# Layer 0 of a two-layer graph network: a buffer of its own for the second table's rows, their split behind the router, loop values loaded a step ahead, and one gate's products behind the turned sums

## The chip, the cores and the metric

The kernel runs on one core of a Trainium2 chip. The metric is the device time of one execution in microseconds (us). An execution is one launch that computes everything below.

## The reference, cut to what matters

There are 6250 nodes with 256 features, and 100,000 edges sorted by their target. The targets are drawn as 6250 times a uniform number squared, so that low node numbers get many more edges than high ones.

```
x = x + GRU(sum over edges of (LN(x)[src] + rel[type]), LN(x))          # layer 0, graph part
x = x + shared_mlp(LN(x)) + top-2-of-4 experts_mlp(LN(x))               # layer 0, feed forward part
x = x + (sum over edges of LN(x)[src]) @ W.T / (degree + 1) + ...       # layer 1, graph part
x = x + top-2-of-8 experts of gelu MLPs on LN(x)                        # layer 1, feed forward part
```

## The kernel before

Nodes are cut into 49 tiles of 128. A table of normalised rows lies in HBM (`table1` for layer 0, `table2` for layer 1). GpSimd (POOL) walks once over the edges in chunks of 128 (784 chunks, four to a block) and gathers one row of the table per edge with an indirect DMA (L763) into `rows`, a ring of 8 blocks. Before a block it waits until TensorE (PE) has used the block that held the slot before (`free`), and it tells PE when blocks have landed (`ready`, L751).

For each tile ("window") VectorE (DVE) builds a one-hot matrix per edge chunk (`dve_onehots`, L789 and L793), and PE multiplies it with the gathered rows and sums into a PSUM bank (`pe_window`, L814 to L836). The number of blocks of a window is data: PE and DVE load it, and the place of the window in the ring, from SBUF into registers (`value_load`) and then run a loop over the blocks. PE needs two loads for a window; DVE needs three for the first 8 blocks of a window, and one with a branch for the blocks behind them (`late`). ScalarE (ACT) and DVE then empty the bank (`act_empty` L1293 and L1296, `dve_empty` L1307).

Tiles are worked on in groups: one tile, then eleven groups of four, then two of two, from the highest tile to the lowest. The dense work of group g-1 is cut into steps d1 to d5, and an order written out by hand (`run_graph`) puts one window of group g behind each of the steps d1 to d4 of group g-1, on every engine the same way. d1 is the GRU (PE turns the sums with L953 and L957, ACT copies them with L1092, and the gate products L934 follow), d2 turns the new state back, adds it to `x_res` and normalises into `h4` (L1224), d3 holds the router and the first two layers of the feed forward part, and d4 its third layer, the second layer norm into `h4` again, and the turning of the next group's `h4_in`. d5 splits that `h4` into two f16 halves in `part`: the high one on ACT (L1151), the low one on DVE (L1281). ACT then sends `part` to `table2` (L1154) and waits for `lo_done` before it does. d5 of group g-2 stands behind the first window of group g, so between d1 and d2 of group g-1.

Each engine runs its own instructions in order. Layer 1 begins behind a barrier that ends layer 0; it gathers from `table2` in the same way with another set of steps.

Of the kernel before, what the change touches and what calls it, by code (L numbers as in the profile page):

```python
# [23 lines left out]
ds = bass.ds  # L24
# [47 lines left out]
def program(nc, a, out):  # L72
# [6 lines left out]
    with ExitStack() as ctx:  # L79
# [25 lines left out]
        place = sb("place", [P, NT * 2], I32)  # L105
        to_list = sb("to_list", [P, LCOLS], I32)
        from_list = sb("from_list", [P, LCOLS], I32)
# [136 lines left out]
        part = sb("part", [P, GW, PARTS * D], F16, layer0)  # L244

# [99 lines left out]
        with nc.Block() as block:  # L345
# [35 lines left out]
            def _(pool):  # L381
# [7 lines left out]
                nc.gpsimd.iota(place[:, :], pattern=[[P, NT], [0, 2]], base=1, channel_multiplier=1)  # L389
# [380 lines left out]

        def dve_onehots(dve, q, t, late):

            if late:
                blocks = dve.value_load(windows[0:1, ds(t + NT, 1)], min_val=1, max_val=PASS + 1)
                with dve.If(blocks > MH):
                    dve_onehots_of(dve, q, t, MH, blocks)
            else:
                dve_onehots_of(dve, q, t, 0, dve.value_load(early[0:1, ds(t, 1)], min_val=1, max_val=MH))

        def dve_onehots_of(dve, q, t, j0, j1):  # L780
            before = dve.snap(window_first(dve, t) + t)
            first = narrow(dve.value_load(windows[0:1, ds(t + 2 * NT, 1)]), 0, PASS)
# [137 lines left out]
        def pe_d1(pe, g, w):  # L920
# [38 lines left out]
            last.then_inc(S["redT_ps"], 1)  # L959

# [23 lines left out]
        def pe_d2(pe, g, w):  # L984
            pe.wait_ge(S["deg_sb"], g + 1)
            for c in range(C):
                pe.wait_ge(S["hnew"], 2 * g + c + 1)
                for half, lo, k in halves(w):
                    for i in range(lo, lo + k):
                        o = (i - lo) * D + c * P  # L990
                        last = nc.tensor.transpose(bank[3 + half][:, o:o + P], nT[:, c, i * P:(i + 1) * P], ident[:, :])
                    if c == C - 1:
                        last.then_inc(S["back_ps"], per_half(w))

        def pe_d3(pe, g, w):
            n = w * P
            for i in range(w):
# [30 lines left out]
        def pe_d4(pe, g, w):  # L1028
            n = w * P
            pe.wait_ge(S["gates_ready"], g + 1)  # L1030
# [116 lines left out]
        def act_d5(act, g, w):  # L1147
            act.wait_ge(S["table2_out"], 16 * g + 16)
            act.wait_ge(S["h2_ready"], g + 1)
            for half, lo, k in halves(w):  # L1150
                nc.scalar.activation(part[:, lo:lo + k, 0:D], h4[:, lo:lo + k, :],  # L1151
                                     ACT.Copy).then_inc(S["hi_done"], per_half(w))
            act.wait_ge(S["lo_done"], CREDIT + 2 * g + 2)
# [20 lines left out]
        def dve_d1(dve, chain, g, w):  # L1174
# [30 lines left out]
        def dve_d2(dve, chain, g, w):  # L1205
# [15 lines left out]
            if not (isinstance(g, int) and g == 0):  # L1221
                dve.wait_ge(S["hi_done"], CREDIT + 2 * g)
# [29 lines left out]
        def dve_d4(dve, chain, g, w):  # L1252
# [20 lines left out]
            ln_apply(first_tile(g), w).then_inc(S["h2_ready"], 1)  # L1273
# [4 lines left out]
        def dve_d5(dve, chain, g, w):  # L1278
            for half, lo, k in halves(w):
                dve.wait_ge(S["hi_done"], CREDIT + 2 * g + half + 1)  # L1280
                nc.vector.tensor_tensor(part[:, lo:lo + k, D:2 * D], h4[:, lo:lo + k, :],  # L1281
# [28 lines left out]
        def nothing(g, w):  # L1310
            return None

# [44 lines left out]
        with nc.Block() as block:  # L1357
# [5 lines left out]
            def _(pe):  # L1363
                pe.sem_inc(q1.used, MH)
                run_graph(lambda g, i: pe_windows(pe, q1, g, i, None),
                          [lambda g, w, f=f: f(pe, g, w) for f in (pe_d1, pe_d2, pe_d3, pe_d4)] + [nothing], pe)

            @block.scalar
            def _(act):
# [4 lines left out]
                run_graph(lambda g, i: act_emptied1(act, g, i),  # L1374
                          [lambda g, w, f=f: f(act, g, w) for f in (act_d1, act_d2, act_d3, act_d4, act_d5)], act)
# [3 lines left out]
            def _(dve):  # L1379
                chain = Chain(dve, "layer0_chain", 64)  # L1380
                for at in (G_ONE, G_AGAIN + E0):
# [3 lines left out]
                run_graph(dve_gather(dve, q1, evacuate1),  # L1385
                          [lambda g, w, f=f: f(dve, chain, g, w) for f in (dve_d1, dve_d2, dve_d3, dve_d4, dve_d5)], dve)
# [5 lines left out]
        ffn = ctx.enter_context(ExitStack())  # L1392

# [75 lines left out]
        low_f = sb("low_f", [P, 2 * GW], F32, layer1)  # L1469
        place_f = sb("place_f", [P, NT * 2], F32, layer1)  # L1470
# [123 lines left out]
        def dve_e3(dve, chain, g, w):  # L1594
# [18 lines left out]
            if isinstance(g, int) and g == 0:  # L1613
                dve.wait_ge(R["cols_ready"], 2)
# [25 lines left out]
        with nc.Block() as block:  # L1640
# [12 lines left out]
            def _(pool):  # L1653

                nc.gpsimd.iota(from_list[:, :], pattern=[[1, LCOLS]], base=0,
# [6 lines left out]
            def _(pe):  # L1662
                pe.sem_inc(q2.used, MH)
                steps = [lambda g, w: pe_e0(pe, g, w), lambda g, w: pe_e1(pe, g, w), lambda g, w: pe_e2(pe, g, w), lambda g, w: pe_e3(pe, g, w), nothing]
# [14 lines left out]
            def _(dve):  # L1679
# [7 lines left out]
                dve.wait_ge(R["cols_ready"], 1)  # L1687
# [4 lines left out]
                chain = Chain(dve, "layer1_chain", 64)  # L1692

# [318 lines left out]
```

## Time and profile before

| what | us |
|---|---|
| median of 3 executions without the profiler | 3396.59 (3394.66 to 3401.94) |
| the profiled execution | 3414.43 |
| its span, from the first to the last instruction | 3412.9 |
| PE busy in the span | 2328.8 |
| POOL busy in the span | 1923.9 |

The profiled execution took 17.8 us longer than the median. All rows below come from it. The first gather of layer 0 starts about 112 us into the span, the last ends at 1472, and layer 1 begins at 1520.7.

### The profile page before, as it was taken

The numbers are of one execution on the slowest core, as the hardware profiler recorded it, in microseconds if no ns is written. First come the engines' busy times: TensorE is split into PE (matmuls) and PEld (weight loads), VectorE is DVE, ScalarE is ACT, GpSimd is POOL, SyncE is SP. The second block draws the span as 40 slices with busy tenths as digits, with TensorE's granted clock in tenths as the row PEclk, the third lists the DMA queues.
The fourth block names the chain that finished last, engine by engine and source line by source line (L and its number), as shares of the span: only waits on it lengthen the run. The fifth ranks groups of instructions, "written<-read, shape, count | busy, mean of one in ns | idle before, by whom it ended". The sixth has DMA issues, their size and how long they took to land. (4 is left out here: it accounts for less than half of the span.)

```text
span 3412.9 us, 47179 instructions
## 1 busy us (share of the span) xinstructions
PE 2328.8 (68%) x11708; PEld 1564.6 (46%) x11709; DVE 1532.5 (45%) x4138; ACT 828.9 (24%) x1644; POOL 1923.9 (56%) x2043
## 2 busy tenths in 40 slices
PE   1478999988866775345666555444443389999996
PEld 1245555555443442132333232221111179999996
DVE  7445555555542433123555443332321156666663
ACT  2233333333322211020110000000000035555543
POOL 0364445556666666626666666666666445555553
PEclk6589999999986776566777766665665589999998
DMA  5322222223232323223333333333333443333334
GB/s 166 88 81 67 71 65 79 79 81 89 87 90 81 87 82 88 82 66 90 101 92 99 92 92 95 90 91 92 91 99 89 138 99 72 73 73 71 71 48 106
DMA packets 163077, 298.23 MB, mean 87 GB/s; under 512 B 47543, under 2 KB 106656, under 8 KB 162752
## 3 DMA queue, kind: packets, MB, share of 16 engines
q0 software_dynamic: 96736, 235.19, 26.3%
q1 hardware_dynamic: 41476, 39.54, 3.7%
q10 hardware_dynamic: 24732, 22.06, 2.1%
q8 instruction: 44, 0.72, 0.1%
q14 instruction: 89, 0.73, 0.1%
HBM read 255.78 MB, written 47.27 MB: 89 GB/s over the span
## 5 line engine op out<-in xcount | busy, mean ns | idle before, releaser
L763 POOL DMA_INDIRECT rows<-table,srcT x1568 | 1552.4, 990 | 985.5 <-issue 498.3
L829 PE MATMUL bank<-rows,onehot 128*128 x1952 | 672.7, 486 | 704.4 <-POOLq L751 435.6
L829 PEld LDWEIGHTS bank<-rows,onehot 128*128 x1952 | 218.6, 112 | 1118.8 <-issue 995.6
L789 DVE SCALAR_TENSOR_TENSOR onehot<-iota_row,tbase,dstT 128x512 f16 x488 | 366.6, 753 | 677.8 <-issue 429.2
L1923 ACT ACTIVATE hid<-bank,b 128x256 f32<-128x256 f32 x432 | 178.9, 465 | 291.5 <-PE bank L1875 266.6
L1873 PE MATMUL bank<-W_high,hid_high 128*128 128x256 f32 x864 | 244.9, 283 | 0.0
L1873 PE MATMUL bank<-xe_high,W_high 128*128 128x256 f32 x864 | 241.2, 279 | 4.8 <-DVE xe_low L1956 4.7
L1874 PE MATMUL bank<-xe_low,W_high 128*128 128x256 f32 x864 | 240.0, 278 | 0.0
L1875 PE MATMUL bank<-xe_high,W_low 128*128 128x256 f32 x864 | 240.0, 278 | 0.0
L1874 PE MATMUL bank<-W_low,hid_high 128*128 128x256 f32 x864 | 239.9, 278 | 0.0
L1875 PE MATMUL bank<-W_high,hid_low 128*128 128x256 f32 x864 | 239.9, 278 | 0.0
L1638 ACT ACTIVATE sums<-bank 128x256 f32<-128x256 f32 x49 | 18.8, 383 | 897.8 <-issue 401.8
L1969 DVE TENSOR_TENSOR hid_low<-hid,hid_high 128x512 fp32r<-128x512 f32 x216 | 150.6, 697 | 168.3 <-ACT hid_high L1927 166.8
L1833 POOL DMA_INDIRECT totals<-ys,to_old x112 | 182.9, 1633 | 73.5 <-POOL to_new L1813 49.2
L1824 POOL DMA_INDIRECT xs<-normal,rows_of x110 | 132.4, 1204 | 64.7 <-POOL rows_of L1820 44.4
L1873 PEld LDWEIGHTS bank<-xe_high,W_high 128*128 128x128 f32 x864 | 163.4, 189 | 6.5 <-issue 6.5
L1874 PEld LDWEIGHTS bank<-xe_low,W_high 128*128 128x128 f32 x864 | 163.5, 189 | 0.0
L1875 PEld LDWEIGHTS bank<-xe_high,W_low 128*128 128x128 f32 x864 | 163.4, 189 | 0.0
L1873 PEld LDWEIGHTS bank<-W_high,hid_high 128*128 128x128 f32 x864 | 162.3, 188 | 0.0
L1874 PEld LDWEIGHTS bank<-W_low,hid_high 128*128 128x128 f32 x864 | 162.3, 188 | 0.0
L1875 PEld LDWEIGHTS bank<-W_high,hid_low 128*128 128x128 f32 x864 | 162.2, 188 | 0.0
L1927 ACT ACTIVATE hid_high<-hid 128x512 fp32r<-128x512 f32 x216 | 136.5, 632 | 7.0
(351 smaller groups left out, 3754.0 us busy)
## 6 DMA issues: line engine op xcount, KB each, us to landing
rows<-table,srcT POOLq DMA_INDIRECT x1568
W<-in_L_ffn_W_dram SPq DMA_DIRECT2D x14, 1024.0 KB
x_res<-in_x_dram SPq DMA_DIRECT2D x1, 6144.0 KB, 22.4
normal<-xn ACTq DMA_DIRECT2D x11, 528.0 KB
table<-part ACTq DMA_DIRECT2D x11, 512.0 KB
totals<-x_res SPq DMA_DIRECT2D x11, 512.0 KB, 6.8
table<-part SPq DMA_DIRECT2D x6, 512.0 KB, 2.9
table<-part_b SPq DMA_DIRECT2D x6, 512.0 KB, 2.9
```

What stands on the lines that cost most here:

```text
L763: nc.gpsimd.indirect_dma_start(out=rows[:, k % (M * U), 0:ROW], out_offset=None, in_=q.table, in_offset=bass.IndirectOffsetOnAxis(srcT[:, ...
L789: last = nc.vector.scalar_tensor_tensor(onehot[:, ds(slot, U), :], iota_row[:, :].unsqueeze(1).to_broadcast([P, U, P]), base, dstT[:, ds(k ...
L829: last = nc.tensor.matmul(acc[:, 0:ROW], hots[:, ds(hot0 + s * P, P)], ring_rows[:, ds(row0 + s * ROW, ROW)], start=False, stop=False, ski ...
L1638: nc.scalar.activation(sums4[:, slot_of(g, i), :], acc[:, 0:D], ACT.Copy).then_inc(R["high_out"], 1)
L1824: nc.gpsimd.indirect_dma_start(out=xs[:, s, :], out_offset=None, in_=normal, in_offset=bass.IndirectOffsetOnAxis(rows_of[:, s:s + 1], axis ...
L1833: nc.gpsimd.indirect_dma_start(out=totals, out_offset=bass.IndirectOffsetOnAxis(to_old[:, s:s + 1], axis=0), in_=ys[:, s, :], in_offset=No ...
L1873: nc.tensor.matmul(acc, w_high, m_high, start=start, stop=False)
L1874: nc.tensor.matmul(acc, w_high, m_low, start=False, stop=False)
L1875: return nc.tensor.matmul(acc, w_low, m_high, start=False, stop=stop)
L1923: nc.scalar.activation(hid[:, hc, :], bank[1 + pair][:, o:o + TT], ACT.Gelu, bias=b1[b][:, hc:hc + 1]).then_inc(X["gelu_done"], 1)
L1927: nc.scalar.activation(hid_high[:, both, :], hid[:, both, :], ACT.Copy).then_inc(X["hid_high"], 1)
L1969: nc.vector.tensor_tensor(hid_low[:, both, :], hid[:, both, :], hid_high[:, both, :].bitcast(F32), ALU.subtract).then_inc(X["hid_ready"], 1)
```

## The change

Six edits, all but the last in layer 0.

- The second layer norm writes into a new buffer `h2_4` and no longer into `h4`; d5 reads it. The wait on `hi_done` moves from the writes of `h4` (L1224) to those of `h2_4`.
- d5 of group g-2 moves from between d1 and d2 of group g-1 to between d3 and d4, behind the third window. The wait for `lo_done` and the DMA to `table2` become a step of their own (d6) behind the fourth window.
- PE loads the two values of each window of the next group ahead: those of window 0 in d1 behind the hidden products, and those of windows 1, 2 and 3 at the head of d2, d3 and d4 (for groups of four tiles).
- DVE loads the three values for the one-hots of window 1 right behind the one-hots of window 0, inside d1.
- The six hidden products of gate r, half 1 (bank 1) move from ahead of the turned sums to behind them.
- The index buffers `place`, `to_list` and `from_list` are taken from SBUF later, and the iota of `place` moves from the kernel's start to the head of layer 1 on POOL.

```
@@ pe_d1
-            for c, gate, b in GATES:
+            for c, gate, b in GATES[0:2]:
                 if (c, gate) == (0, 1):
                     pe.wait_ge(S["hT_sb"], g + 1)
                 products(bank[b][:, 0:n], gate * D + c * P, (hidden,), True, False, ...)
+            if not (isinstance(g, int) and g == LAST) and size(g + 1) == GW:
+                q1.window_ahead.window(first_window(g + 1) + 0)
...
             last.then_inc(S["redT_ps"], 1)
+            products(bank[1][:, 0:n], P, (hidden,), True, False)
@@ pe_d2 (pe_d3 and pe_d4 the same with + 2 and + 3)
+            if not (isinstance(g, int) and g == LAST) and size(g + 1) == GW:
+                q1.window_ahead.window(first_window(g + 1) + 1)
             pe.wait_ge(S["deg_sb"], g + 1)
@@ pe_window
-            first = window_first(pe, t)
-            blocks = pe.value_load(windows[0:1, ds(t + NT, 1)], min_val=1, max_val=PASS + 1)
+            known = q.window_ahead.take(t)
+            if known is None:
+                q.window_ahead.window(t)
+                known = q.window_ahead.take(t)
+            first, blocks = known
@@ dve_d1
                 dve_onehots(dve, q1, first_window(g) + w, False)
+                if size(g + 1) > 1:
+                    q1.hot_ahead.onehots(first_window(g) + w + 1)
@@ dve_d2
-            if not (isinstance(g, int) and g == 0):
-                dve.wait_ge(S["hi_done"], CREDIT + 2 * g)
@@ dve_d4
-            ln_apply(first_tile(g), w).then_inc(S["h2_ready"], 1)
+            dve.wait_ge(S["hi_done"], CREDIT + 2 * g)
+            ln_apply(first_tile(g), w, h2_4).then_inc(S["h2_ready"], 1)
@@ act_d5, dve_d5: h4 becomes h2_4
+        def act_d6(act, g, w):
             act.wait_ge(S["lo_done"], CREDIT + 2 * g + 2)
             act.dma_start(table2[...], part[:, 0:w, :]).then_inc(S["table2_out"], 16)
+        def run_layer0(gather, steps, behind):
+            gather(0, 0)
+            for g in range(1, LAST + 2):
+                at = {LAST - 1: {0: 0, 2: 1}, LAST: {0: 0, 3: 1}, LAST + 1: {}}.get(g, {i: i for i in range(GW)})
+                for i in range(GW):
+                    steps[i](g - 1, size(g - 1))
+                    if i in at:
+                        gather(g, at[i])
+                    if g >= 2 and i in behind:
+                        behind[i](g - 2, size(g - 2))
+            for i in sorted(behind):
+                behind[i](LAST, size(LAST))
@@ ACT: behind = {2: act_d5, 3: act_d6}, DVE: behind = {2: dve_d5}, PE: behind = {}
@@ POOL, head of layer 1
+                nc.gpsimd.iota(place[:, :], pattern=[[P, NT], [0, 2]], base=1,
+                               channel_multiplier=1).then_inc(R["cols_ready"], 1)
                 nc.gpsimd.iota(from_list[:, :], ...).then_inc(R["cols_ready"], 1)
```

## Rows read from the trace of the kernel before

**Rows 1.** Busy time per stretch of 100 us (busy us and instructions, PEclk, DMA share, GB/s).
```profile
300.00:400.00 100.00, 89.22 (x395) 55.64 (x395) 55.00 (x141) 35.82 (x70) 42.36 (x42) 0.95 0.21 61
...
1300.00:1400.00 100.00, 52.82 (x163) 26.56 (x163) 28.31 (x86) 12.75 (x28) 61.56 (x62) 0.59 0.30 88
```
**Rows 2.** Who POOL waited for, 100 to 1520 us.
```profile
POOL rows L763 <- PE bank L833: 122.5, 28, 15.5
```
**Rows 3.** Timeline of POOL: some gathers that waited for PE.
```profile
754.10 1.17 POOL L763 DMA_INDIRECT rows<-table,srcT  x1 [2.61 <-PE bank L833]
...
1269.90 0.94 POOL L763 DMA_INDIRECT rows<-table,srcT  x1 [4.07 <-PE bank L833]
```
**Rows 4.** Who PE waited for, 200 to 900 us (total, times, longest).
```profile
PE bank L829 <- issue: 15.9, 37, 1.9
...
PE bank L934 <- ACT split_parts L1092: 9.4, 8, 1.2
...
PE bank L1000 <- DVE h L1224: 7.2, 5, 1.8
```
**Rows 5.** Timeline of PE in one group, 604 to 686 us.
```profile
608.42 0.63 PE L934 MATMUL bank<-split_parts,whhT_high 128*128 128x512 f32 x2
608.89 1.95 PE L953 MATMUL bank<-unscale,red 128*128 128x128 f32 x16
...
613.73 0.73 PE L934 MATMUL bank<-split_parts,wihT_high 128*128 128x512 f32 x2 [1.18 <-ACT split_parts L1092]
...
634.13 0.39 PE L818 MATMUL bank<-zeros 128*128 128x512 f16 x1 [0.15 <-ACT counts L1296]
635.71 1.03 PE L829 MATMUL bank<-rows,onehot 128*128 x4 [1.18 <-DVE typehot L793]
...
642.11 0.18 PE L836 MATMUL bank<-zeros 128*128 128x16 f16 x1
643.79 1.78 PE L1000 MATMUL bank<-ident,h 128*128 128x128 f32 x8 [1.50 <-DVE h L1224]
```
**Rows 6.** Timeline of DVE in the same group.
```profile
606.27 0.42 DVE L1307 TENSOR_TENSOR red<-red,bank 128x256 f32<-128x256 f32 x1 [1.51 <-ACT red L1293]
...
634.35 0.75 DVE L789 SCALAR_TENSOR_TENSOR onehot<-iota_row,tbase,dstT 128x512 f16 x1 [2.31 <-issue]
...
638.52 1.29 DVE L1281 TENSOR_TENSOR part<-h,part 128x512 f16<-128x512 f32 x2
...
673.30 0.42 DVE L1307 TENSOR_TENSOR red<-red,bank 128x256 f32<-128x256 f32 x1 [1.75 <-ACT red L1293]
```
**Rows 7.** Timeline of ACT in the same group.
```profile
672.35 0.59 ACT L1135 ACTIVATE split_parts<-bank 14x512 fp32r<-14x512 f32 x1 [3.66 <-issue]
```
**Rows 8.** Timeline of DVE and PE in an earlier group, at 393 us.
```profile
393.05 0.69 DVE L1198 TENSOR_TENSOR work<-work 128x512 f32<-128x512 f32 x1
...
395.09 0.39 PE L814 MATMUL bank<-zeros 128*128 128x512 f16 x1 [0.64 <-issue]
```
**Rows 9.** Timeline of PE: one long wait for nothing that the profile shows.
```profile
1263.69 0.80 PE L934 MATMUL bank<-split_parts,wihT_high 128*128 128x256 f32 x2 [4.48 <-issue]
```
**Rows 10.** Timeline of all engines at the end of layer 0.
```profile
1481.61 0.51 PE L934 MATMUL bank<-split_parts,wihT_high 128*128 128x256 f32 x2 [0.75 <-ACT split_parts L1092]
...
1509.37 0.36 ACT L1135 ACTIVATE split_parts<-bank 14x256 fp32r<-14x256 f32 x1
...
1515.27 0.30 ACT L222 ACTIVATE stdev<-mean_var,eps_scaled 128x2 f32<-128x2 f32 x1 [2.57 <-DVE mean_var L205]
...
1516.65 0.63 ACT L1151 ACTIVATE part<-h 128x512 f16<-128x512 f32 x1 [1.09 <-DVE h L215]
1518.11 0.37 ACTq L1154 DMA_DIRECT2D table<-part  x1
1520.72 0.47 POOL L1655 IOTA from_list<- 128x410 int32 x1 [48.77 <-POOLq L1357]
```
**Rows 11.** Groups of POOL by line, the whole span (count, busy, mean ns).
```profile
L389 POOL IOTA place<- 128x98 int32 x1 | 0.4, 361 | 0.0
```

More of the change, by code:

```diff
@@ L769, in pool_chunks, with __init__, onehots, window @@
                         ready(i, 1 if i < BLOCKS - 1 else 1 + PASS - BLOCKS)
+        class Ahead:
+            def __init__(self, eng):
+                self.eng, self.loaded = eng, {}
+            def onehots(self, t):
+                self.loaded[t] = (self.eng.value_load(early[0:1, ds(t, 1)], min_val=1, max_val=MH),
+                                  self.eng.snap(window_first(self.eng, t) + t),
+                                  narrow(self.eng.value_load(windows[0:1, ds(t + 2 * NT, 1)]), 0, PASS))
+            def window(self, t):
+                self.loaded[t] = (window_first(self.eng, t),
+                                  self.eng.value_load(windows[0:1, ds(t + NT, 1)], min_val=1, max_val=PASS + 1))
+            def take(self, t):
+                return self.loaded.pop(t, None)
         def dve_onehots(dve, q, t, late):
@@ L775, in dve_onehots, with dve_onehots_of @@
                 with dve.If(blocks > MH):
-                    dve_onehots_of(dve, q, t, MH, blocks)
+                    dve_onehots_of(dve, q, t, MH, blocks, None)
             else:
[L778 to L782, printed above, removed]
+                known = q.hot_ahead.take(t)
+                j1 = known[0] if known else dve.value_load(early[0:1, ds(t, 1)], min_val=1, max_val=MH)
+                dve_onehots_of(dve, q, t, 0, j1, known)
+        def dve_onehots_of(dve, q, t, j0, j1, known):
+            if known:
+                before, first = known[1:]
+            else:
+                before = dve.snap(window_first(dve, t) + t)
+                first = narrow(dve.value_load(windows[0:1, ds(t + 2 * NT, 1)]), 0, PASS)
             base = tbase[:, ds(t, 1)]
@@ L996, in pe_d3 @@
             n = w * P
+            if not (isinstance(g, int) and g == LAST) and size(g + 1) == GW:
+                q1.window_ahead.window(first_window(g + 1) + 2)
             for i in range(w):
@@ L1029, in pe_d4 @@
             n = w * P
+            if not (isinstance(g, int) and g == LAST) and size(g + 1) == GW:
+                q1.window_ahead.window(first_window(g + 1) + 3)
             pe.wait_ge(S["gates_ready"], g + 1)
@@ L1364, in _ @@
                 pe.sem_inc(q1.used, MH)
-                run_graph(lambda g, i: pe_windows(pe, q1, g, i, None),
-                          [lambda g, w, f=f: f(pe, g, w) for f in (pe_d1, pe_d2, pe_d3, pe_d4)] + [nothing], pe)
+                q1.window_ahead = Ahead(pe)
+                run_layer0(lambda g, i: pe_windows(pe, q1, g, i, None),
+                           [lambda g, w, f=f: f(pe, g, w) for f in (pe_d1, pe_d2, pe_d3, pe_d4)], {})
             @block.scalar
@@ L1380, in _ @@
                 chain = Chain(dve, "layer0_chain", 64)
+                q1.hot_ahead = Ahead(dve)
                 for at in (G_ONE, G_AGAIN + E0):
@@ L1384, in _ @@
                 normalised(dve, 0, 1)
[L1385 to L1386 removed]
+                run_layer0(dve_gather(dve, q1, evacuate1),
+                           [lambda g, w, f=f: f(dve, chain, g, w) for f in (dve_d1, dve_d2, dve_d3, dve_d4)],
+                           {2: lambda g, w: dve_d5(dve, chain, g, w)})
         layer0.close()
         ffn = ctx.enter_context(ExitStack())
+        to_list = sb("to_list", [P, LCOLS], I32, ffn)
+        from_list = sb("from_list", [P, LCOLS], I32, ffn)
         W1 = sb("W1", [P, C, H], F32, ffn)
@@ L1469, in program @@
         low_f = sb("low_f", [P, 2 * GW], F32, layer1)
+        place = sb("place", [P, NT * 2], I32, layer1)
         place_f = sb("place_f", [P, NT * 2], F32, layer1)
@@ L1692, in _ @@
                 chain = Chain(dve, "layer1_chain", 64)
+                q2.hot_ahead = Ahead(dve)
                 run_graph(dve_gather(dve, q2, evacuate2),
```

19 lines of the change are left out of this document (9 added, 10 removed).

## The prediction

> **What bounds the kernel now.** I read the stretches of 100 us first. Layer 0 falls into two halves. Until about 770 us PE is busy 89 us in 100 and POOL only 42 to 59; from there on POOL stays at about 62 in 100 while PE drops to 53 [rows 1]. A busy share of 62 is POOL at its own limit: it issues 62 gathers in that time and, as its timeline shows, stops only for rows to land and never for PE, but once. The view of who POOL waits for says how the two halves are tied. It waits 122.5 us in 28 waits for a ring slot that PE has to give back [rows 2]. Nearly all of it, 115 us, lies in the waits before 755 us; the last of them is 2.61 us long at 754, and behind it there is one more of 4.07 us at 1270 [rows 3]. So up to 755 us a microsecond taken from PE is a microsecond less that POOL waits, and since POOL is never let go of afterwards, it reaches the end of layer 0. Behind 770 us nothing that PE saves counts, up to the last gather at 1472 us. Then the last group's steps lie open until 1520.7 [rows 10]. Layer 1 and the experts are not touched, save for one iota.
>
> Next, who PE waits for in the PE-bound half [rows 4]: 9.4 us for ACT's copy of the turned sums in 8 waits, 7.2 us for DVE's `h4`, and 15.9 us of short waits on nothing visible inside the window loops. A group takes about 80 us, and 7 groups run their d1 and d2 before 755 us. The rest is read in one of them.
>
> **The change part by part.**
>
> *Gate products behind the turned sums.* ACT's copy leaves PE idle 1.18 us between L957 and the first input product [rows 5]. The six products that move there take about 1.4 us (two start 0.47 us ahead of what follows them at 608.42, so 0.23 us each). They were work anyhow, so the gap is filled and 1.2 us is saved per group. The turned sums start 1.4 us sooner; what they need (the last window emptied by DVE at 606.69, against a start at 608.89) is there [rows 5, 6]. Bounds: 0.8, if the sums then wait a little, and 1.3.
>
> *d5 out of the way of d2.* On DVE the chain from the last gate product to `h4` has no slack: L1203, 2.31 us of gap, four blocks of one-hots, the emptying, L1281 for 1.29 us, then the adds, the statistics and L1224, for which PE waits 1.50 us at 643.79 [rows 5, 6]. L1281 goes: 1.29 us. In its new place DVE has a gap of 1.75 us ahead of the emptying of window 2, and ACT one of 3.66 us ahead of the gate copy L1135, in which the high half (1.15 us) finds room [rows 6, 7]. So it costs nothing there; without this cover it would be 1.29 us per group, on DVE's way to the third layer's low halves. The removed wait on `hi_done` ended nothing in any of the 49 writes of `h4`. The DMA moves to ACT's idle time behind window 3. ACT waited about 4 us per group for DVE's low half; the square root it holds up waits for DVE's statistics anyway, so that stall is worth nothing.
>
> *DVE's three loads.* They sit in the 2.31 us gap with the late load, its branch and the loop's start [rows 6]. No row shows a load by itself. Their price lies between nothing and the whole 2.31. PE gives the nearest row: from the end of L1198 at 393.74 to L814 at 395.09 are 1.35 us, which hold the issue of half the turns and two loads [rows 8]; I take 0.45 us for a load, some 1.3 us for three, and count 1.2. They move to where DVE's next instruction feeds a product that PE reaches about 3 us later, so they are hidden.
>
> *PE's loads.* A pair costs about 0.9 us by the same row. Ahead of window 1 it vanishes under a wait. But the pair of window 2 now stands ahead of L1000, and that of window 3 ahead of the gate rows' turn, both where PE's issue has no lead, since it just left a loop bound by issue: the short waits of 0.3 us per block there show it [rows 4]. So I count: window 2 and 3 gain their short waits (0.9 us together), and the pair ahead of the gate turn takes the same 0.9 back. Net nothing, between -0.9 and +0.9 us per group.
>
> *Together up to `h4`.* Window 1 needs the counts of window 0, there at about 634.1, so its first block can start at 634.5 instead of 635.71 and its loop ends at 641.1 instead of 642.3 [rows 5]. Behind it come 0.9 us of loads: 642.0. `h4`, now there just before L1000 starts at 643.79, is ready 2.5 us sooner, at about 641.2. So L1000 starts at 642.0 and not 643.79: 1.8 us. Bounds: 1.3 (L1281 alone) and 2.7 (loop's end without loads).
>
> [...]
>
> *Sum of the PE-bound half.* 1.2 + 1.8 + 0 = 3.0 us per group, times 7 is 21.0, less 1.0 for the first full group, whose wait for `h4` is only 0.6 us: 20.0 us. POOL has 115 us of waits there to give, but the last is 2.61 us, a little short of one group's 3.0.
>
> *The wait at 1270.* It stems from a PE chain of d1 work with a gap of 4.48 us in it [rows 3, 9]. PE comes there about 1 us sooner: -1.0 us, between 0 and -4.1.
>
> *The tail.* The filler saves 0.75 us [rows 10]. But d5 of group 12 now stands between d3 and d4 of the last group, where ACT has no gap: its 0.63 us delay L1135, and DVE's half (0.69 us, the same size as at the end) then delays the spread products: about +1.0 us. And d6 of group 12 now comes behind the last square root at 1515.57. The high half of the last group waits for that DMA: it lands as the last one does, within 2.6 us of its issue (1518.11 to the barrier at 1520.7), so about 1517.9 and not 1516.65 [rows 10]: +1.25 us. Tail: -0.75 + 1.0 + 1.25 = +1.5 us.
>
> *Layer 1.* The iota of `place`, 0.36 us, stands ahead of POOL's first gather there [rows 11]: +0.4 us. At the kernel's start it was hidden 100 us ahead of the first gather.
>
> Sum: -20.0 - 1.0 + 1.5 + 0.4 = -19.1 us. Against the profiled execution (3414.4, its span 3412.9) that is 3395.3. The median without profiler is 17.8 us lower, so 3377.5.
>
> **Rivals.**
>
> 1. *The loads give back what the rest wins.* If PE's pairs for windows 2, 3 and 0 all lie open (2.7 us per group) and DVE's loads are worth little, a group gains 1.2 + 1.3 + 0.9 - 2.7 = 0.7 us: 5 us in seven groups, 3 after the tail: 3394, no change that shows. For it: PE has no lead behind a loop bound by issue. Against it: in d1 it has one, since PE waits for nothing between its last products and the window behind d1.
> 2. *Slower.* One mechanism, PE's register loads: each pair costs 1.35 us (all of rows 8) and all four lie open, 5.4 us per group against 2.5 + 0.9 gained: +2 us per group, 14 in seven, 16 with tail and iota: 3412. It decides from about 0.85 us per pair with all four open. Against it: the load of window 1 already stood behind a wait and now stands under one.
> 3. *Code moves, and a stall with it.* PE has lone gaps of 4 to 5 us on "issue", as at 1263.69 [rows 9]. If one of these falls newly into the PE-bound half, or two do, the gain is 5 to 9 us smaller: 3382 to 3387. [...]
> 4. *More than counted.* If the loads cost PE nothing, every step reaches its upper bound: 1.3 + 2.7 + 0.9 = 4.9 us per group, 34 in seven. With all of the 4.07 at 1270 and less 1.9 for tail and iota that is 36 us: 3360. For it: both waits that it closes stand in every group. Against it: the two bounds of PE's loads are free only with a lead.
>
> **How the numbers follow.** Chances: forecast 0.64, the stall 0.13, more 0.07, loads give back 0.11, slower 0.05. A measurement of this kernel can tell 0.2%, 6.8 us, from no change: faster means below 3389.8. All of the forecast's, the stall's and the larger gain's mass lies there, except some 0.04 of its lower edge: faster 0.80, same 0.15, slower 0.05. The range 3360 to 3391 runs from rival 4 to just above the bound, where the group gains 1.3 us.
>
> **What would show it.** In the profile after: no PE wait on L1092 in front of L934 in the groups before 755 us; L1281 ahead of L1255 and no longer ahead of L1210; DVE's gap ahead of window 1's one-hots near 1.1 instead of 2.31 us; L1000's wait for `h4` gone or owed to issue; POOL's waits for PE down by about 20 us from 122.5; the last gather of layer 0 near 1451 instead of 1472; a tail of about 50 instead of 48.8 us. The prediction is wrong if PE shows new gaps ahead of L1000, L1032 or L953 of 1 us or more, or if POOL's saved waits come back as waits for landing.

## The result, and the profile after

The changed kernel takes 3364.0 us (median of 5, 3358.94 to 3374.91) against 3396.59 before (median of 5, run beside it). The ratio is 0.9908, with a 95% interval from 0.9890 to 0.9926: 32.6 us less, where 19.1 were forecast. Later it ran in two more sets of runs, on chips 10 and 8, beside the kernel before; the record names no chip for the first set. There it was 15.7 and 15.5 us faster by the medians, and 16.7 and 19.5 by the ratios (0.9951 [0.9936, 0.9967] and 0.9943 [0.9923, 0.9963]). So the forecast lies between what the sets gave, and this spread is itself something to explain.

The first profiled execution took 3374.91 us, 10.9 above its median; its span is 3373.4, so 39.5 under the span before. (The record doesn't say on which chip the profiled execution of the kernel before ran. It is none of the five above, and 17.8 us longer than their median, so part of this difference may not be the change's.) Where the 39.5 us lie: the last gather of layer 0 ends at 1427.91 instead of 1471.94 (-44.0), the tail up to layer 1 is 52.17 us instead of 48.78 (+3.4), and the rest of the span is 1.1 us longer. So everything was won ahead of the last gather. PE turns the ninth group's `h_in` at 716.5 instead of 764.0, 47.5 us sooner, and 44.0 of these reach the last gather.

The view of who POOL waited for, 100 to 1520 us of the changed kernel (total, times, longest), answers [rows 2]:

```profile
POOL rows L760 <- DMA rows<-table,srcT: 254.3, 100, 4.3
POOL rows L760 <- issue: 233.4, 687, 6.8
...
POOL rows L760 <- PE bank L857: 66.6, 18, 14.2
```

122.5 us in 28 waits have become 66.6 in 18. That is 55.9 less. Waits for landing rose from 235.6 to 254.3, so part of the freed time was lost to rows that had not landed. Before 760 us POOL's last large wait for PE is now at 670.0 instead of 754.1, which means that POOL is let off earlier, and behind that it has but one wait of more than 0.4 us, at 1227. The stretches of 100 us show the same, against [rows 1]:

```profile
300.00:400.00 100.00, 91.52 (x373) 53.02 (x373) 58.63 (x176) 38.91 (x76) 53.25 (x54) 0.93 0.26 75
1300.00:1400.00 100.00, 34.68 (x75) 9.94 (x75) 12.45 (x28) 0.00 (x0) 61.05 (x63) 0.50 0.28 81
```

In the first of them POOL is busy 53 instead of 42 us. In the second it is at its own limit of 61, as before.

Who PE waited for, 200 to 900 us, against [rows 4]:

```profile
PE bank L853 <- POOLq L748: 24.4, 9, 6.8
PE bank L1031 <- DVE h L1259: 8.2, 7, 1.5
PE bank L1072 <- ACT split_parts L1168: 6.1, 9, 0.7
PE bank L1037 <- ACT work L1147: 5.0, 9, 0.6
PE bank L853 <- DVE typehot L814: 4.9, 12, 0.7
PE bank L853 <- issue: 4.8, 16, 0.4
PE bank L979 <- issue: 2.8, 6, 0.6
```

L853 is L829 of before, L1031 is L1000, L1259 is L1224, L1072 is L1039. The wait for ACT's copy of the turned sums (9.4 us before) is gone. The short issue waits in the window loops fell from 15.9 to 4.8. L1031 still waits for DVE's `h4`, 8.2 us in 7 waits. (Before, the view names 7.2 in 5; two more, 4.2 us, it puts down to "issue", and each of these ended 0.06 us behind the end of a part of `h4`, so it was 11.4 us in 7.) The new waits ahead of L979 (the turned sums) are PE's loads for window 0. The 24.4 us at the top stand behind 756 us, where POOL is the bound.

The same group as in [rows 5] now turns its sums 38 us sooner. PE, from its timeline:

```profile
570.71 2.02 PE L979 MATMUL bank<-unscale,red 128*128 128x128 f32 x16 [0.57 <-issue]
...
573.88 1.04 PE L958 MATMUL bank<-split_parts,whhT_high 128*128 128x512 f32 x2
574.76 0.63 PE L958 MATMUL bank<-split_parts,whhT_low 128*128 128x512 f32 x2
575.23 0.63 PE L958 MATMUL bank<-split_parts,whhT_high 128*128 128x512 f32 x2
575.69 0.66 PE L958 MATMUL bank<-split_parts,wihT_high 128*128 128x512 f32 x2
...
603.68 1.09 PE L1031 MATMUL bank<-ident,h 128*128 128x128 f32 x8 [0.95 <-DVE h L1259]
```

The six hidden products stand behind the turned sums, and the first input product at 575.69 follows with no gap, where [rows 5] have 1.18 us. DVE in the same group, against [rows 6]:

```profile
577.87 0.75 DVE L810 SCALAR_TENSOR_TENSOR onehot<-iota_row,tbase,dstT 128x512 f16 x1 [0.97 <-issue]
...
582.95 0.75 DVE L1224 SCALAR_TENSOR_TENSOR work<-bank,bhh,work 128x512 f32<-128x512 f32 x1 [1.14 <-issue]
...
594.64 0.75 DVE L810 SCALAR_TENSOR_TENSOR onehot<-iota_row,tbase,dstT 128x512 f16 x1 [0.70 <-PE bank L857]
...
629.01 1.29 DVE L1317 TENSOR_TENSOR part<-h,part 128x512 f16<-128x512 f32 x2
630.21 0.68 DVE L1290 TENSOR_TENSOR split_parts<-work,split_parts 128x512 fp32r<-128x512 f32 x1
```

The gap of 2.31 us ahead of window 1's one-hots is 0.70; the three loads now lie open for 1.14 us ahead of L1224 (10.3 us in 9 such gaps from 140 to 760 us, so 1.15 each), where nobody waits for them. The low half, 1.29 us, stands between d3 and d4.

The tail, from the timelines of ACT, its queue and DVE, against [rows 10]:

```profile
1465.19 0.62 ACT L1184 ACTIVATE part<-h 128x512 f16<-128x512 f32 x1
1465.71 0.36 ACT L1168 ACTIVATE split_parts<-bank 14x256 fp32r<-14x256 f32 x1
...
1476.03 0.63 ACT L1184 ACTIVATE part<-h 128x512 f16<-128x512 f32 x1 [1.92 <-DMA table<-part]
1477.49 0.37 ACTq L1189 DMA_DIRECT2D table<-part  x1
```
```profile
1465.91 0.69 DVE L1317 TENSOR_TENSOR part<-h,part 128x512 f16<-128x512 f32 x1 [1.90 <-ACT part L1184]
1466.52 0.42 DVE L1290 TENSOR_TENSOR split_parts<-work,split_parts 128x256 fp32r<-128x256 f32 x1
```

ACT's high half delays the gate copy L1168, DVE's low half delays the spread products (L1290), and the last high half waits 1.92 us for the DMA before it: the two delays that the tail's sum names.

### The profile page after: what moved, and what is told of

It is laid out like the page before. It is cut to its first block and busy times, and to the rows that moved or that the text cites. A ratio compares the mean times of both kernels' runs of the same rounds, so it can differ in the third digit from the quotient of the medians.

```text
span 3373.4 us, 47180 instructions
## 1 busy us (share of the span) xinstructions
PE 2324.7 (69%) x11708; PEld 1570.8 (47%) x11709; DVE 1528.6 (45%) x4138; ACT 828.3 (25%) x1644; POOL 1917.8 (57%) x2043
## 5 line engine op out<-in xcount | busy, mean ns | idle before, releaser
L853 PE MATMUL bank<-rows,onehot 128*128 x1952 | 666.7, 483 | 742.4 <-POOLq L748 686.7
L853 PEld LDWEIGHTS bank<-rows,onehot 128*128 x1952 | 217.1, 111 | 1144.1 <-issue 1007.0
L1697 ACT ACTIVATE sums<-bank 128x256 f32<-128x256 f32 x49 | 18.7, 382 | 907.0 <-PE bank L860 907.0
L1937 PEld LDWEIGHTS bank<-xe_low,W_high 128*128 128x128 f32 x864 | 163.3, 189 | 0.0
```

Of the source, the lines that this page charges most:

```text
L853: last = nc.tensor.matmul(acc[:, 0:ROW], hots[:, ds(hot0 + s * P, P)], ring_rows[:, ds(row0 + s * ROW, ROW)], start=False, stop=False, ski ...
L1937: nc.tensor.matmul(acc, w_high, m_low, start=False, stop=False)
```

## The experiments

Every ratio is to the kernel before on the same chip, with its 95% interval. Four kernels that ran together share the chip. The kernel before itself took 3408.9, 3421.5 and 3421.1 us on the three chips used here, and 3396.6 in the first set of runs. Where a gain by the medians and one by the ratio differ, both are given.

### First chip of these runs: each edit taken back

**again** is the changed kernel unchanged.

> The changed kernel once more, as the mark for the three runs beside it on the same chip. All theories: 0.988 to 0.994 of before, some 32 us faster.

3393.20 us, 0.9951 [0.9936, 0.9967]: 15.7 us faster, not 32.6, so this expectation failed. Its last gather ends at 1444.52, 16.6 us later than in the first trace of the same program.

**no_filler** puts the six products back ahead of the sums.

```
-            for c, gate, b in GATES[0:2]:
+            for c, gate, b in GATES:
...
-            products(bank[1][:, 0:n], P, (hidden,), True, False)
```

> The changed kernel with gate r's six hidden products back ahead of the turned sums. Theory A (each edit saves its own term, the filler 1.2 us per group in 8 groups and 0.75 in the tail): 9 to 10 us slower than the changed kernel, and the wait of 1.18 us on L1125 is back in each PE-bound group. Rival (the filler's gap would be passed on to the next wait for DVE): under 3 us slower.

3398.24 us, 0.9964 [0.9951, 0.9977]: 5.0 us more than again. Between the two expectations, and the intervals overlap. In its trace PE's wait for ACT's copy is back in five of the seven groups (5.9 us, up to 1.2). only_filler below tests the same edit from the other side.

**no_pe_ahead** takes PE's four loads back into the windows (the four `q1.window_ahead.window(...)` go).

> The changed kernel with each window's two values loaded by PE at the window again. Theory A (prediction: what the windows win, the pairs ahead of L1031 and L1065 give back): within 3 us of the changed kernel. Theory B (PE's loads carry most of what the sum lacked): 12 to 18 us slower, with short issue waits of 0.3 us and the lone ones of 1 to 3 us back in front of L853 and L838. Theory C (where the code lies): the same long issue waits may come or go at other places, with no order by window.

3389.58 us, 0.9939 [0.9921, 0.9957]: 3.6 us less than again, by overlapping intervals. The loads bring nothing, or cost a little; theory B's 12 to 18 us are excluded. The wait ahead of the turned sums (L979 in the changed kernel) is what they cost visibly: 0.35 to 0.57 us per group.

**no_dve_ahead** takes DVE's three loads back.

```
-                if size(g + 1) > 1:
-                    q1.hot_ahead.onehots(first_window(g) + w + 1)
```

> The changed kernel with DVE's three values of window 1 loaded behind the late branch again. Theory A: DVE's gap there grows by about 1.2 us per group and PE waits that much longer for h4: 7 to 9 us slower. Rival (PE's own loop bounds window 1, not DVE): under 3 us slower.

3394.38 us, 0.9949 [0.9930, 0.9968]: 1.2 us more than again. By the medians theory A's 7 to 9 us are missed by 6; the two intervals alone would just allow 7, and only_dve below excludes it. Yet the loads are in the trace. Who PE waited for, 200 to 740 us, first this kernel and then the changed one (its first trace):

```profile
PE bank L853 <- DVE typehot L814: 12.3, 8, 2.4
```
```profile
PE bank L853 <- DVE typehot L814: 4.4, 10, 0.7
```

PE waits 8 us longer for the second window's one-hots, and the stretch from the end of the first window to L1031 adds up to 75.4 us in seven groups, against 62.3 and 67.2 in the two traces of the changed kernel. But the stretch behind it, from L1031 to the end of the third window, is 173.6 us against 178.6 and 178.4. So by these traces 5 us come back behind d2, and that is the question which the third set takes up. It is a small difference for single traces: the same stretch is 183.3 us in again2, a third trace of the changed kernel.

### Second chip: d5, a better version, and code moved without work

**again2** is the changed kernel once more.

> The changed kernel once more, as the mark for the other three of this call. Theory A (the change saves about 3 us per group, and the rest of what was measured is how long unnamed stalls happen to last in an execution): a ratio between 0.991 and 0.9955 again, 15 to 30 us. In the trace, waits of PE of 0.7 us and more on nothing visible between 143 and 760 us: anything from 2 us in all (the first trace after) to 19 us (the second one). Rival (the unnamed stalls are a fixed property of the program): 16 such waits and some 18 us again, as in the second trace, and 0.995.

3405.91 us, 0.9943 [0.9923, 0.9963]: 15.5 us faster, 19.5 by the ratio. Between 143 and 773 us its trace has 16 PE waits of 0.7 us and more that the profile puts down to nothing visible, 19.5 us in all, and again has 13, 14.6 us. The first trace had two, 2.0 us. Both expectations hold this, the rival's (16 waits, some 18 us) more closely. What the label is worth is asked further down.

**d5_early** puts d5 and d6 back between d1 and d2, with the buffer kept.

```
-                           {2: lambda g, w: act_d5(act, g, w), 3: lambda g, w: act_d6(act, g, w)})
+                           {0: lambda g, w: (act_d5(act, g, w), act_d6(act, g, w))})
...
-                           {2: lambda g, w: dve_d5(dve, chain, g, w)})
+                           {0: lambda g, w: dve_d5(dve, chain, g, w)})
```

> The changed kernel with d5 and the DMA step back behind the first window, so between d1 and d2, the buffer of its own kept. DVE's low half (1.29 us) stands ahead of the emptying on the way to the normalised rows of d2 again. Theory A (the move is worth most of 1.3 us per group, since DVE ends d2): 6 to 9 us slower than the changed kernel in layer 0, with the last group's tail about 2 us shorter: 4 to 7 us in all. Rival (PE's window loop and its issue bound that stretch, DVE has slack; leaving DVE's loads behind cost only 1 us where 7 to 9 were expected): within 2 us of the changed kernel, or up to 2 faster by the tail.

3406.01 us, 0.9952 [0.9933, 0.9970]: 0.1 us more than again2 by the medians, 3 by the ratios. That is the rival's number and not theory A's 4 to 7, though the intervals overlap too far to exclude either. Who PE waited for, 200 to 740 us, shows d5's delay nevertheless, as 12.2 us in 6 waits with a longest of 2.6, against 8.2 in 7 and 1.5 in the first trace of the changed kernel (with the waits ahead of L1031 that are put down to "issue", 14.6 us here and 8.6 in again2):

```profile
PE bank L1031 <- DVE h L1259: 12.2, 6, 2.6
```

**best** is the changed kernel with PE's loads ahead for window 1 alone, and group 12's d5 and d6 early in the tail.

```
-            if not (isinstance(g, int) and g == LAST) and size(g + 1) == GW:     # in d1, d3 and d4
-                q1.window_ahead.window(first_window(g + 1) + ...)
...
+                    if g == LAST + 1 and i == 0:
+                        for k in sorted(behind):
+                            behind[k](g - 2, size(g - 2))
-                    if g >= 2 and i in behind:
+                    if 2 <= g <= LAST and i in behind:
```

> The changed kernel, with PE's loads ahead kept for the second window alone (the one that stands in front of a wait), and with d5 and the DMA step of the last group but one behind d1 of the last group. Theory A: the loads for windows 0, 2 and 3 cost PE some 0.5 us per group (3.6 us in the run that took all four back), and the tail loses the 0.6 us high half, the 0.7 us low half and most of the 1.9 us wait for the DMA: 4 to 7 us faster than the changed kernel, tail 46.5 to 47.5 us instead of 48.3 to 52.2. Rival (the loads are within noise, and only the tail moves): 1.5 to 3 us faster.

3398.59 us, 0.9923 [0.9898, 0.9949]: 22.9 us faster than before, and 7.3 less than again2, though the intervals overlap. The tail is 47.82 us against 48.65 in again2 and 49.04 in again: 1 us of it, and longer than the 46.5 to 47.5 expected.

**pad_after** has 48 increments of a semaphore that nobody waits for at the head of layer 0 on PE, ACT and DVE.

```
+                for _ in range(48):
+                    pe.sem_inc(S["pad"], 1)      # act and dve the same
```

> The changed kernel with 48 semaphore increments, on a semaphore that nobody waits for, at the head of layer 0 on PE, ACT and DVE alike, ahead of all of their work there and well ahead of the first window's rows. No work is changed, only where the code lies. Theory A (the stalls on nothing visible do not hang on small shifts of the code, but on the execution): within 3 us of the changed kernel. [...]

3406.83 us, 0.9946 [0.9927, 0.9965]: as again2. The waits on nothing visible stayed (16 of 0.7 us and more on PE, 18.3 us). Moving the code by so much did not move the time (3406.83 us against 3405.91). This tests no larger shift.

### Third chip: one edit alone on the kernel before

**only_filler** is the kernel before with the six products behind the sums.

> The kernel before with one edit alone: the six hidden products of gate r, half 1, behind the turned sums. Theory A (ACT's copy leaves a gap of 1.2 us per group there, and nothing else takes the gap's place): 7 to 9 us faster than before, ratio 0.9974 to 0.998; in the trace no wait of PE's products on ACT's copy in the PE-bound half. Rival (the products that come early also cover the wait of the turned sums for the last window's emptying, so the gap moves there): under 3 us faster, with waits of 0.3 to 1.3 us ahead of the turned sums.

3412.64 us, 0.9966 [0.9955, 0.9976]: 8.5 us faster by the medians, 11.6 by the ratio (8.2 to 15.4 by its interval). That is theory A's size or somewhat more, and the rival's "under 3" is excluded. PE's waits on ACT's copy, 200 to 740 us, fell from 7.1 us in 6 to 1.9 in 3, and 2.4 us in two waits stand newly ahead of the turned sums: a small part of the rival's mechanism.

**only_d5** is the kernel before with the buffer and the moved d5 and d6, and with them the index buffers' new place and the iota at the head of layer 1.

```
-            ln_apply(first_tile(g), w).then_inc(S["h2_ready"], 1)
+            dve.wait_ge(S["hi_done"], CREDIT + 2 * g)
+            ln_apply(first_tile(g), w, h2_4).then_inc(S["h2_ready"], 1)
...
+                           {2: lambda g, w: dve_d5(dve, chain, g, w)})
```

> The kernel before with the buffer of its own for the second norm's rows, d5 behind the third window and the DMA step behind the fourth (and the iota at the head of layer 1, which SBUF's room asks for). Theory A (DVE's chain to the normalised rows loses 1.3 us per group and PE waits for it): PE's waits for these rows near zero, the stretch from the end of the first window to d2 1.2 us shorter than before, 9 us less in seven groups, 2 us given back in the tail: 6 to 7 us faster than before. Rival (with d5 late or early the changed kernel took the same time, so what follows d2 absorbs it): that stretch is shorter all the same, but the time is within 3 us of before, since the stretch behind d2 grows by as much.

3411.24 us, 0.9971 [0.9959, 0.9984]: 9.9 us faster by the medians, 5.5 to 14 by the interval. PE's waits for `h4` fell to 1.5 us in 4 waits, from 7.2 in 5 [rows 4]. From the end of the first window to d2 it is 73.7 us in seven groups against 79.7 before. Theory A holds and its rival does not. Yet d5_early, which takes the same move back out of the changed kernel, cost 0.1 to 3 us only: what a move is worth alone and what its loss costs beside the other edits are two numbers. The tail is 49.4 us, 0.6 longer.

**only_dve** is the kernel before with DVE's loads ahead and the buffer of its own, d5 left where it was.

> The kernel before with DVE's three loads of the second window a step ahead, the buffer of its own kept but d5 left between d1 and d2. Theory A (1.2 us per group on the same chain): 6 to 8 us faster than before, PE's waits for the second window's one-hots and for the normalised rows together 8 us less. Rival (taking the loads back cost the changed kernel 1 us only): within 3 us of before.

3421.92 us, 1.0002 [0.9987, 1.0017]: nothing gained, at most 4.4 us. The rival is right. From the end of the first window to d2 it saves the most of the three, 70.6 us against 79.7, and it waits 11.5 us for `h4`. Behind d2, up to the end of the third window, it takes 192.1 us against 184.1.

**best2** is best once more.

> The kernel of the run called best once more, on this chip: the changed kernel with PE's loads ahead kept for the second window alone and d5 of the last group but one early. Theory A: 0.990 to 0.9945 of before again, so 19 to 34 us, more than the changed kernel's 15.5 and 15.7 on the two other chips of these runs. Rival (the first result was the spread of the executions): 0.9945 or more, the changed kernel's own ratio.

3400.43 us, 0.9940 [0.9923, 0.9958]: 20.7 us faster. In both runs best is ahead of what the changed kernel reached in the later sets, by 5 to 7 us in the medians, and in neither is it separated from it by the intervals. It is the version to keep; that it beats the changed kernel isn't shown.

### Two readings across the traces

*What comes back behind d2.* PE's clock is part of it. The stretches of 1 us around d2 in the same group, in the changed kernel and in only_d5 (busy us of PE, PEld, DVE, ACT and POOL, then the granted clock):

```profile
306.00:307.00 1.00, 0.00 (x0) 0.00 (x0) 0.60 (x5) 0.83 (x3) 0.65 (x1) 1.00 0.00 0
308.00:309.00 1.00, 0.55 (x4) 0.20 (x2) 0.05 (x1) 0.53 (x2) 0.00 (x0) 1.00 0.43 127
309.00:310.00 1.00, 0.88 (x6) 0.88 (x6) 0.25 (x1) 0.56 (x2) 0.57 (x1) 0.74 0.00 0
310.00:311.00 1.00, 1.00 (x7) 1.00 (x6) 0.87 (x3) 0.00 (x0) 0.69 (x2) 0.50 0.00 0
315.00:316.00 1.00, 1.00 (x3) 0.48 (x2) 0.00 (x0) 0.00 (x0) 0.89 (x1) 0.50 0.45 131
316.00:317.00 1.00, 1.00 (x4) 0.41 (x3) 0.00 (x0) 0.93 (x2) 0.66 (x1) 0.84 0.34 94
```
```profile
315.00:316.00 1.00, 0.35 (x4) 0.11 (x2) 0.00 (x0) 0.96 (x3) 0.70 (x2) 1.00 0.19 49
318.00:319.00 1.00, 0.82 (x4) 0.47 (x5) 0.88 (x3) 0.00 (x0) 0.00 (x0) 1.00 0.43 127
319.00:320.00 1.00, 0.62 (x4) 0.13 (x3) 1.00 (x4) 0.00 (x0) 0.00 (x0) 0.74 0.07 21
320.00:321.00 1.00, 1.00 (x3) 0.39 (x3) 1.00 (x3) 0.00 (x0) 0.67 (x1) 0.50 0.00 0
322.00:323.00 1.00, 1.00 (x4) 0.39 (x3) 0.95 (x6) 0.00 (x0) 0.00 (x0) 0.56 0.41 119
323.00:324.00 1.00, 0.66 (x4) 0.20 (x2) 0.61 (x3) 0.52 (x2) 0.59 (x1) 1.00 0.00 0
```

In both the granted clock falls from its upper level (1.00) to its lower (0.50) behind microseconds in which PE was busy for only 0.35 to 0.88, or not at all; that this idle time is what lowers it isn't shown. In only_d5 this falls on the window loop, in front of d2, and is over at 323. In the changed kernel the clock is still 1.00 from 305 to 309, PE is idle for 306 to 307, and the lower level falls on 310 to 316, which is d3, made of dense products. PE's timelines give the price: the first eight products of L1045 take 5.69 us in the changed kernel, 0.71 each,

```profile
312.26 5.69 PE L1045 MATMUL bank<-work,sW 128*128 128x512 f32 x8
```

and the same eight in only_d5 3.68 us, 0.46 each,

```profile
327.99 3.68 PE L1038 MATMUL bank<-work,sW 128*128 128x512 f32 x8
```

and from the first of them to the end of that block of products it is 12.5 us against 10.5. The granted clock is 0.50 from 312 to 316, 0.84 in the next microsecond and 1.00 from 317 in the first, and 1.00 throughout in the second. So where a wait ahead of d2 went, the stretch at 0.50 came to lie on products that take longer in it. The granted clock of all seven groups says the same. The table gives the time at the lower level (twice what the granted clock lacks to 1.00, times the length of the stretch), ahead of d2 and behind it:

| kernel | first window's end to d2, us | d2 to third window's end, us |
|---|---|---|
| before | 13.9 | 50.9 |
| only_dve (with the loads ahead) | 0.3 | 64.5 |
| no_dve_ahead (without them) | 17.1 | 23.9 |
| again (with them) | 0.7 | 40.2 |

In both pairs DVE's loads ahead take 13.6 to 16.4 us of the lower clock away ahead of d2, and 13.6 to 16.3 more of it lie behind d2. The four kernels without these loads have 13.7 to 17.1 us ahead of d2, the ten traces with them 0 to 1.7, but for 6.8 in best2. If all the work in such time took twice as long as at 1.00, half of the time would be lost: by these numbers an upper estimate of 6.8 to 8.2 us. The stretch behind d2 grew by 8.0 us in the first pair and by 4.9 in the second. So the place where the lower clock falls is shown. That it is all of what comes back isn't: the stretch behind d2 alone spreads from 178.5 to 183.3 us over three traces of one program.

*Why the same program took 16.6 us longer to its last gather.* A warning on a label comes first. "Issue" and "remote" say that the profile found no event that ended a wait, and not that nothing did. The wait of 4.48 us in [rows 9] is one: PE started at 1263.69, 0.05 us behind this step of DVE, for which it had waited,

```profile
1263.17 0.47 DVE L1187 SCALAR_TENSOR_TENSOR work<-bank,bhh,work 128x256 f32<-128x256 f32 x1
```

and in the changed kernel the profile names the same wait:

```profile
1220.96 0.80 PE L958 MATMUL bank<-split_parts,wihT_high 128*128 128x256 f32 x2 [5.67 <-DVE work L1224]
```

The first trace of the changed kernel has few such labels and the others many. Of ACT's waits of 1.5 us and more between 143 and 773 us, 20 have one in the kernel before, 21 in again, 27 in again2 and none in the first trace; but ACT's wait of 2.30 us at 163, which the first trace puts down to DVE, is counted for again and again2, where it is just as long. So these counts, and those of PE's waits above, don't measure lateness.

A start is late if it comes well behind the end of what it needs. The first copy of the sums by ACT in the first full group shows it. In the changed kernel's first trace, the window's end on PE and then the copy:

```profile
168.04 0.17 PE L860 MATMUL bank<-zeros 128*128 128x16 f16 x1
```
```profile
168.34 0.38 ACT L1329 ACTIVATE red<-bank 128x256 f32<-128x256 f32 x1 [5.01 <-PE bank L860]
```

and in again2, the same instructions of the same program:

```profile
168.86 0.17 PE L860 MATMUL bank<-zeros 128*128 128x16 f16 x1
```
```profile
171.44 0.38 ACT L1329 ACTIVATE red<-bank 128x256 f32<-128x256 f32 x1 [7.20 <-remote]
```

0.13 us behind PE in the one, 2.41 in the other, with ACT idle since 163.3 and 164.2. In the kernel before it is 2.18 us, in again 1.50. The time was not lost on ACT. By the trace's semaphore events, the semaphore with which PE reports this window is raised at 168.25 in the first trace, 0.04 us behind the end that the profile gives for L860, but at 170.45 in again and at 171.35 in again2, 1.42 and 2.32 us behind it; ACT starts 0.08 to 0.09 us after it in all three. So PE's report is late. The profile's ends of matmuls are modelled, and whether the product itself was late can't be told from it.

Counting the time in which ACT was idle behind the end of its input, the first trace has no copy that starts over 0.6 us late among 34 of them up to 770 us. The kernel before has three (8.4 us), again six (11.6 us), again2 six (15.1 us), and each of the ten other kernels two or more. Three places repeat in most of the traces, the copies at about 170, 370 and 450 us, and their lengths differ: at the first it is 0.7 to 4.4 us.

## Why the prediction was right, point by point

- **The number**: the sum was 19.1, and the two later sets gave 15.7 and 15.5 us by the medians, 11 to 26 by their intervals. The first set's 32.6 holds some 13 us that stand in no term of the sum; that it still fell inside the range, near its lower end, is luck.
- **The bound** was read rightly: PE up to where POOL is let off, then POOL. The gain stands at the ninth group's start, and 3.5 us of it were lost up to the last gather.
- **The filler**, 1.2 us per group, 8.4 in seven: only_filler gave 8.5 by the medians and 8.2 to 15.4 by the interval. no_filler lost 5.0.
- **The step up to `h4`**, 1.8 us per group: from the end of the first window to d2 the seven groups take 79.7 us before, 62.3 in the first trace of the changed kernel, 67.2 in again and 68.5 in again2, so 2.5, 1.8 and 1.6 us less per group. The sum is right and its parts are not. DVE's loads, counted at 0.5, bring 1.3 there (only_dve against before) and 1.2 (again against no_dve_ahead). d5, counted at 1.3, brings 0.9 (only_d5) and 0.4 (again2 against d5_early, 71.0 us).
- **What bounds that step** was wrong: PE's loads were to end it, with `h4` there before. In the first trace PE still waits for `h4` in all seven groups, 1.2 us each. In again PE's loads end it in two groups, at 619.67 and 701.07, where `h4` had been there for 1.2 us.
- **d5 out of the way** was worth some 9 us in seven groups by the bound for L1281 alone, less the tail. only_d5 gave 9.9 [5.5, 14]. In its new place no cost can be read: from the third window's end to the fourth's the seven groups take 96.1 us before and 92.8, 97.3 and 101.8 in the three traces of the changed kernel.
- **DVE's three loads** are as long as estimated: 1.15 us against 1.2, by the new gap ahead of L1224. But alone they gave nothing (-4.4 to +5.8 us by the interval). The saving reaches d2 and isn't seen behind it.
- **PE's loads, net 0 (between -0.9 and +0.9 per group)**: having them cost 3.6 us over not having them by the medians, 0.5 us per group, so inside. The cost that shows is 0.35 to 0.57 us ahead of L979, and about 1.0 ahead of L1031 in the two groups just named: a gap of 1.15 and 1.18 us, where no_pe_ahead has 0.15 (at 624.44).
- **The sum of the PE-bound half**, 20: the parts measured alone make 8.5 + 9.9 - 0.8 = 17.6 by the medians with the tail in it, and the changed kernel 15.6 in the two later sets. But taken back one at a time, the four edits cost 5.0 - 3.6 + 1.2 + 0.1 = 2.7 us only. So the gains don't simply add: with three edits in place the fourth is worth less than alone. No run shows where it goes, and each of these four differences is inside its interval.
- **The wait at 1270**: 4.07 became 2.88 (now at 1227), -1.2 against -1.0. The gap of 4.48 us in the PE chain that it stems from was a wait for DVE, which had eight blocks of one-hots to build first.
- **The tail**: the delays by d5 and by the DMA are in the rows; the tail grew by 3.4 us in the first trace against 1.5, but -0.1 and +0.3 in again2 and again. In the first trace PE ran d4 behind its 1.34 us wait at a granted clock of 0.50, from 1467 to 1471 (0.63 us for a pair of L1079, against 0.40 for one of L1046 before, at 1.00).
- **Rival 3, a stall moves with the code**, had no ground in [rows 9], whose gap is that wait for DVE. In the padded kernel no time changes. The late reports of PE exist all the same, and differ between executions of one program. **Rival 4, more than counted**, gave 36 us from loads that are free. The first set's 32.6 is near it in size, yet the profile of that set shows another thing: the late starts are missing in it, and between 143 and 760 us PE is idle for 47.0 us, against 60.3 in again, 69.0 in again2 and 75.7 before. That this is the cause of the difference between the sets is argued from one trace of each, not shown.
- **The signs**: no PE wait for ACT's copy, L1281's new place and DVE's gap (0.70 us) came out as said. The wait for `h4` did not go away. The numbers hang on the trace: POOL's waits for PE fell by 55.9, 32.3 (again) and 6.8 us (again2), where 20 was forecast, and the last gather ends at 1427.91, 1444.52 and 1464.58, where 1451 was forecast. Of the signs of being wrong, POOL's waits for landing rose by 18.7 us in the first trace, a third of what was freed, by 3.1 in again and not in again2. PE has new waits of over 1 us ahead of L979, for DVE (1.3 us in again, 1.5 in again2), and one of 2.5 us ahead of L1065 in again2; the first trace has none.

What stays open is why the profile of the first set was free of late starts, and whether its other executions were. Chip, place of the program in memory and chance can't be told apart, since no kernel here controls any of them.

## What to carry to other kernels

Price a step both where it is taken out and where its work lands: alone, the filler and the moved d5 gave what their rows said within the intervals, while the loads were priced to 0.05 us and still brought nothing. Test an edit from both sides, alone on the kernel before and taken back from the changed one: here the two differ. Look at the granted clock in the stretch behind a saving too: with DVE's loads ahead, 9.1 us were saved ahead of d2 in only_dve, 8.0 us more were spent behind it, and 13.6 us more of the lower clock lay there. And when a result exceeds the sum of its own waits, run the same program again in another set before looking for the cause in the change. Before you call a wait "issue" a stall, look at when the instruction's inputs ended.

## What the runs showed of the hardware

- ACT's copies of the sums start 0.6 to 4.7 us behind the modelled end of their input at a few places in 13 of 14 traces, of different lengths in different traces of one program. At the first of these places PE's semaphore is what comes late, by 1.42 us in again and 2.32 in again2. What delays it isn't shown. The two queues whose kind the page gives as instruction (44 packets with 0.72 MB on q8, 89 with 0.73 MB on q14) show nothing there: again has no packet on them between 131.5 and 170.6 us, and the padded kernel, whose copy is 1.86 us late at 171.3, none between 163 and 193.
- Where DVE's loads are moved ahead, the granted clock of PE falls to its lower level (0.50) behind d2 instead of ahead of it, 13.6 to 16.3 us more of it in seven groups. Eight products of 128x512 took 5.69 us, 0.71 each, where it was 0.50 for some four of these microseconds (the first trace of the changed kernel, at 312), and 3.68 us, 0.46 each, at 1.00 (only_d5, at 328).
- A register load costs DVE about 0.38 us with the register work beside it: three lie open for 10.3 us in 9 gaps between 140 and 760 us, 1.15 each, if nothing else is in them. Its own record in the first trace of the changed kernel is 0.30 us (medians of L731 and L776, 0.31 for L778), and on PE 0.30 too (L731); the prediction took 0.45. Without the loads (no_dve_ahead) five of the eight gaps there are 0.04 us or less, and the other three are longer waits put down to "remote". On PE two cost about 1.0 us, by the gaps of 1.15 and 1.18 us against 0.15.
- The kernel before took 3396.6, 3408.9, 3421.5 and 3421.1 us in its four sets of runs, up to 0.7% apart: as much as the change is worth.
